# Attention in a decoder layer: four bodies written out, and each step's products regrouped (scores and maxima in front, the value product once for 512 columns)

## The reference, cut to what matters

```python
attn = jnp.einsum('bhqd,bhkd->bhqk', q, k) * scale
attn = jax.nn.softmax(attn, axis=-1)
out = jnp.einsum('bhqk,bhkd->bhqd', attn, v)
```

## Time and profile before

| | |
|---|---|
| median of 3 runs | 1193.57 us (1189.91 to 1193.67) |
| profiled execution: span from first to last instruction | 1188.0 us |
| PE busy | 1086.0 us, 91% of the span |
| DVE busy | 1021.9 us, 86% |
| ACT busy | 767.9 us, 65% |
| POOL busy | 352.7 us, 30% |
| DVE maximum reductions (line 812) | 1024, 627.1 us |
| ACT exponentials (line 750) | 512, 520.4 us |

### The profile page before, as it was taken

The page is one execution under the profiler, slowest core; times in us unless marked ns, Lnnn a source line. Parts: engine busy times, 40 slices in busy tenths (PEclk is TensorE's granted clock), DMA queues, the critical chain, the costliest instruction groups (busy, mean ns, idle before and its releaser), DMA issues. The chain is left out here.

```text
span 1188.0 us, 24515 instructions
## 1 busy us (share of the span) xinstructions
PE 1086.0 (91%) x8540; PEld 596.5 (50%) x8540; DVE 1021.9 (86%) x2168; ACT 767.9 (65%) x932; POOL 352.7 (30%) x316
## 2 busy tenths in 40 slices
PE   7889989999999998999999999999994059999998
PEld 6776333333333333333333333337784038888897
DVE  8999889999999998999999999827998975766663
ACT  4552368888888886788887888874555014655653
POOL 2657812202220220222022000022100022876575
PEclk9987699999999999999999999999998559999999
DMA  6786664504422440442344000036432022555433
GB/s 238 250 266 219 150 106 97 95 19 78 75 58 38 84 75 19 78 74 45 51 80 78 17 16 16 17 102 211 157 128 95 0 71 57 150 144 132 111 111 36
DMA packets 84695, 114.10 MB, mean 96 GB/s; under 512 B 25056, under 2 KB 57568, under 8 KB 84576
## 3 DMA queue, kind: packets, MB, share of 16 engines
q1 hardware_dynamic: 66256, 69.82, 19.8%
q0 software_dynamic: 15024, 36.17, 17.2%
q10 hardware_dynamic: 3296, 6.56, 1.6%
HBM read 73.31 MB, written 38.27 MB: 94 GB/s over the span
## 5 line engine op out<-in xcount | busy, mean ns | idle before, releaser
L812 DVE TENSOR_REDUCE b_max_halves<-banks 128x1 f32<-128x512 f32 x1024 | 627.1, 680 | 19.9 <-PE banks L880 19.7
L750 ACT ACTIVATE b_probs<-banks 128x1024 f32<-128x1024 f32 x512 | 520.4, 1026 | 153.9 <-PE banks L931 153.8
L880 PE MATMUL banks<-b_k,b_q 62*128 62x512 f32 x1024 | 399.8, 471 | 5.8 <-DVE b_max_halves L812 1.7
L931 PE MATMUL banks<-b_q,b_k 64*128 64x512 f32 x1024 | 386.9, 457 | 8.4 <-DMA b_q<-b_max_rows 5.2
L902 PE MATMUL banks<-b_probs,b_v 128*17 128x256 f32 (+1 forms) x3840 | 316.3, 402 | 0.2 <-ACT b_probs L750 0.2
L931 PEld LDWEIGHTS banks<-b_q,b_k 64*128 64x128 f32 x1024 | 157.1, 186 | 229.7 <-issue 173.3
L880 PEld LDWEIGHTS banks<-b_k,b_q 62*128 62x128 f32 x1024 | 162.2, 190 | 40.4 <-DVE b_max_halves L812 37.4
L902 PEld LDWEIGHTS banks<-b_probs,b_v 128*17 128x17 f32 x3840 | 64.0, 95 | 166.1 <-issue 99.0
L551 POOL TENSOR_TENSOR b_att<-b_out,b_rec_spread 128x512 f32<-128x512 f32 x32 | 41.0, 1283 | 307.6 <-DMA b_rec_spread<-reciprocals 307.4
L483 POOL DMA_DIRECT2D b_q<-q_stacks x60 | 31.8, 532 | 234.6 <-PE banks L902 220.9
L1851 DVE TENSOR_TENSOR e_hTl<-e_hT,e_hTh 128x512 fp32r<-128x512 f32 x64 | 47.6, 745 | 48.2 <-ACT e_hT L1605 46.6
(11 more groups left out here) (259 smaller groups left out, 1480.5 us busy)
## 6 DMA issues: line engine op xcount, KB each, us to landing
e_w<-in_w SPq DMA_DIRECT2D x16, 1024.0 KB
q_stacks<-a_parts SPq DMA_DIRECT2D x32, 256.0 KB, 4.3
k_stacks<-a_parts SPq DMA_DIRECT2D x32, 256.0 KB, 4.1
b_q<-q_stacks POOLq DMA_DIRECT2D x30, 256.0 KB, 5.7
b_k<-k_stacks POOLq DMA_DIRECT2D x30, 256.0 KB, 6.4
v_tiles<-a_v ACTq DMA_DIRECT2D x8, 544.0 KB, 3.5
b_rec_spread<-reciprocals SPq DMA_DIRECT2D x128, 32.0 KB, 1.8
attended<-b_att SPq DMA_DIRECT2D x128, 32.0 KB, 1.8
```

The source lines that it names most:

```text
L750: nc.scalar.activation(pr[:, S % NP, u], ps[:, 2 * u:2 * u + 2, :], ACT.Exp, scale=D ** -0.5).then_inc(s_ex[u], 1)
L812: v.tensor_reduce(mxp[:, (k // NB) % 2, s, p, t, kh:kh + 1], ps[:, bank(last), :], AX.X, ALU.max)\
L880: nc.tensor.matmul(ps[:, bank(last), :], qs[g][stack, p, at:at + P], ks[g][stack, p, CH * kh:CH * kh + CH], start=True, stop=True).then_in ...
L931: return nc.tensor.matmul(ps[:, 2 * u + s, :], ks[g][stack, u, P * kt:P * kt + P], qs[g][stack, u, CH * h:CH * h + CH], start=True, stop=True)
```

## The change

It does three things, in `attend` alone.

1. `bodies` writes all four batch rows out in Python; no loop is left on any engine.
2. `values` loses its `half`: each step's value product is one group for all 512 columns, for step S - 1, at the end of step S.
3. The order in a step becomes: both scores of u = 0; four maxima; both scores of u = 1; the value product of the step before; then, once in a head group, the transposed maxima as before.

```diff
         def bodies(eng, body):
-            body(0, True, False)
-            with eng.Fori(1, B - 1) as i:
-                body(i, False, False)
-            body(B - 1, False, True)
+            for i in range(B):
+                body(i, i == 0, i == B - 1)
...
-            def values(i, S, half):
+            def values(i, S):
...
-                if kt == 0 and half == 0:
-                    return
                 if kt == 0:
                     pe.wait_ge(s_oe, 8 * i + hg)
-                if kt == 0 or half == 0:
-                    for u in range(2):
-                        pe.wait_ge(s_ex[u], 64 * i + S + 1)
-                at = slice(0, CH) if kt == 0 else slice(HC * half, HC * half + HC)
+                for u in range(2):
+                    pe.wait_ge(s_ex[u], 64 * i + S + 1)
                 for j in range(G):
-                    last = nc.tensor.matmul(ps[VW * j:VW * j + VS, PV, at], vs[hg // 2][:, kt, j, :],
-                                            pr[:, S % NP, j // 2, j % 2, at], start=(kt == 0),
-                                            stop=(kt == KT - 1 and half == 1))
-                if half:
-                    last.then_inc(s_pv, 1)
+                    last = nc.tensor.matmul(ps[VW * j:VW * j + VS, PV, :], vs[hg // 2][:, kt, j, :],
+                                            pr[:, S % NP, j // 2, j % 2, :], start=(kt == 0), stop=(kt == KT - 1))
+                last.then_inc(s_pv, 1)
...
-                def earlier(S, back, half):
-                    if S >= back:
-                        values(i, S - back, half)
+                def earlier(S):
+                    if S:
+                        values(i, S - 1)
                     elif not first:
-                        values(i - 1, KT * NH + S - back, half)
+                        values(i - 1, KT * NH - 1)
...
+                        pe.wait_ge(s_ex[0], 64 * i + S)
+                        for s in range(2):
+                            last_score = scores(g, h, S, 0, s)
+                        last_score.then_inc(s_st[0], 1)
                         for u in range(2):
-                            pe.wait_ge(s_ex[u], 64 * i + S)
-                            scores(g, h, S, u, 0)
                             for x in range(2):
                                 ring(hg, kt, u, x)
-                            scores(g, h, S, u, 1).then_inc(s_st[u], 1)
-                            if u == 0:
-                                earlier(S, 2, 1)
-                            else:
-                                earlier(S, 1, 0)
+                        pe.wait_ge(s_ex[1], 64 * i + S)
+                        for s in range(2):
+                            last_score = scores(g, h, S, 1, s)
+                        last_score.then_inc(s_st[1], 1)
+                        earlier(S)
                         ring(hg, kt, 2, 0)
             bodies(pe, body)
-            values(B - 1, KT * NH - 2, 1)
-            values(B - 1, KT * NH - 1, 0)
-            values(B - 1, KT * NH - 1, 1)
+            values(B - 1, KT * NH - 1)
```

## The result

The changed kernel takes 1340.29 us (median of 4 runs, 1338.24 to 1341.19), beside 1191.74 us before (4 runs; the forecast started from the first three, 1193.57): a ratio of 1.125 (95% interval 1.122 to 1.127), 149 us more. The forecast was 1339.

A forecast was written before the change was run, and what follows sets the result against it. The prediction took PE as the bound by a hair, DVE right behind. Terms +155 - 8.5 - 3 + 2 = +145 us on 1188.0 gave 1333.5, with 5.6 to the median 1339 us; range 1308 to 1370.

The forecast's parts named there:

- What bounds the kernel before: Plain half-step of the attention stage: PE needs 1.21 us, DVE 1.19; the loop's body costs nothing, only its ends.
- The chain of the ring: Three banks tie PE and DVE: reduction and hand-over 0.75, scores 0.65, value product 0.98, next scores 0.77; 3.15 us a step.
- cross-check: The same wait already seen once in the kernel before, 2.71 us, to which the change adds score pairs of 0.22 and 0.24.
- A head group: 8 steps of 3.15 plus 0.26 for transposed maxima: 25.4 us against 20.3, +5.1; over 30.5 groups +155 us.
- The sum: All terms together +145 us on the profiled 1188.0, so 1333.5; with 5.6 to the median, 1339 us.
- Last twelve steps: Steps without maxima: PE 1.63, ACT 1.8, step between 1.8 and 2.15 us; -2 to +2 us, taken as 0.
- Written-out bodies: Loop's jump gone, -7.1 us, entry and exit about 0.8 and 0.6: together -8.5 us, lower bound of the gain 0.
- Start of the stage: Wait for copied rows at the first head group's end mostly covered, -3 us; first steps at half clock, +2 us.
- rival 2: Clock falls as PE idles: 5.0 us a step, about 1800 us throughout, 1490 if a third of steps; chance 0.07.
- Rival 1: Three banks carry DVE over the gap, so DVE sets 20.1 us a head group: about 1176 us; chance 0.06.
- Rival 3: Scores' weights load under the waiting maximum and the value product: 2.93 us a step, about 1288 us; chance 0.08.

The follow-up runs named there:

- straight_only: Kernel before with only its four batch rows written out, its order unchanged: 1182.45 us, ratio 0.994 to the kernel before.
- half_reduce: Changed kernel whose reductions read only every second of the 512 columns: 1275.67 us, ratio 1.070 to the kernel before.
- half_values: Changed kernel whose value products do 256 of 512 columns except at kt = 0: 1254.85 and 1296.81 us; run again, median 1270.19 us.
- fourth_last: Changed kernel with a step's fourth maximum moved behind the scores of u = 1, before the value product: 1283.47 us, ratio 1.080 to the kernel before.
- maxima_apart: Changed kernel with the maxima back in two pairs, each between two scores, value product still one group: 1248.97 us, ratio 1.050 to the kernel before.
- looped: Changed kernel with the loop put back over the two middle batch rows: 1344.82 us, ratio 1.130 to the kernel before.
- four_banks: Changed kernel without the second score product of u = 1, its bank given to the ring: 1200.07 and 1210.13 us, ratio 1.011 to the kernel before.

## Why the prediction was right, point by point

- **What bounds the kernel before** (PE by a hair, DVE right behind, the loop's body free): `straight_only` keeps 20.3 us a head group, so written-out code neither helps nor hurts inside a batch row. That is shown. That PE and not DVE sets the pace is read from 1.21 and 1.19 us a half-step, and no run tells the two apart.
- **The chain of the ring.** The prediction's four terms were 0.75, 0.65, 0.98 and 0.77; the profile has 0.75, 0.67, 0.99 and 0.77 (3.15 against 3.17 a step between the exponentials). The prediction's own cross-check, 2.71 + 0.22 + 0.24, gives 3.17; it did not ask where the 0.02 between the two lay. The terms were then moved: the reduction by -0.27 (`half_reduce`, step -0.27), the value product by -0.43 (`half_values`, step -0.43), the scores' place by -0.22 (`fourth_last`, step -0.24), and both pairs of scores with the maxima's places in `maxima_apart` (2.70 forecast and measured). A fourth bank takes the tie away (20.95 us a head group, nearly DVE's pace). Shown.
- **A head group**: 25.4 forecast, 25.58 measured; 5.27 more than before instead of 5.1 is, over 30.5 head groups, 5 us more than I had. The 0.26 us for the transposed maxima are right (3.42 us in that step). Among the large terms this is the only one that was off by anything that shows.
- **The sum.** On the spans it was +145 forecast and 1339.4 - 1188.0 = 151.4 measured, so the terms together were 6 us too low, 5 of them the chain's 0.02 us a step. That the median came within 1.3 us is partly luck: the kernel before has 5.6 us between its profile's span and the median that I used, the changed kernel only 0.9 (1340.29 - 1339.4).
- **Last twelve steps** at 0: from the start of the last but one head group to the last copy of the value bank it is 39.2 us after (906.3 to 945.5) and 36.1 before (758.7 to 794.8), and four of its steps with maxima explain 4 x 0.72 = 2.9 of the 3.1. Right.
- **Written-out bodies** at -8.5: in the changed kernel's profile every head group at the end of a batch row has the plain length (25.6 us at 317.9 and at 522.5), so all of the 8.5 was got, but not all of it by writing the bodies out. In `straight_only` the gain is 6.3 in the medians, because there the ends keep 0.6 us each, by the wait in `free` shown above. `looped` has plain ends with the loop in place: it is the new order that takes these 0.6 us away, and the loop's own share is the 7.8 us at its jump. That they vanish into the time in which DVE is idle anyway is argued, not shown.
- **Start of the stage** at -1 in all, which is about what it was, by other amounts. The first exponential came 3.9 us earlier (131.3 for 135.2), and the 1.3 us that the second head group had over a plain one went. The first head group took 33.1 us for 24.6, 3.2 more than the 5.3 of any other, though the wait of 2.9 us for the copied rows vanished from it: half clock lasted until 154.5 us of the span, over almost five steps of 5.0 us and not one or two. -3.9 - 1.3 + 3.2 = -2.0. These steps, by PE's timeline:

```profile
138.85 0.79 PE L923 MATMUL banks<-b_q,b_k 64*128 64x512 f32 x2
...
140.85 0.79 PE L878 MATMUL banks<-b_k,b_q 62*128 62x512 f32 x1 [0.36 <-DVE b_max_halves L810]
...
142.00 1.91 PE L896 MATMUL banks<-b_probs,b_v 128*17 128x512 f32 x8
143.84 0.79 PE L923 MATMUL banks<-b_q,b_k 64*128 64x512 f32 x2
```

From scores to scores it is 4.99 us; rival 2 had priced a step at half clock at 5.0.
- **Rival 1** (the ring does not tie) is refuted for this ring, and `four_banks` shows a condition under which it nearly holds (four banks, and one score product less). **Rival 3** (weights loaded under the waiting maximum, 2.93 a step) did not happen: the step is 3.17. What did happen in its direction is a change of partner: the score on the other rows of the array is issued together with the fourth maximum (405.07, in the timeline of the changed kernel), the one on the same rows after it. The block still takes two pairs' time.
- **Rival 2** (the clock) did not happen in the plain steps, but it is near: with a value product half as long TensorE stayed at half clock until 279 us of the span, 125 us longer than in the changed kernel's profile. Its chance of 0.07 was not too much.

## What to carry to other kernels

When a consumer on another engine is as busy as the producer, the buffers between them must last through the longest thing that the producer does in one piece. Three banks give DVE 3 x 0.60 = 1.8 us of work from the moment a bank is free. The next product that it can start on arrives 0.07 + 0.67 + 0.99 + 0.77 = 2.50 us after that moment in the changed kernel and 0.07 + 0.43 + 0.98 + 0.54 = 2.02 in `maxima_apart`, and DVE's idle times, measured as 0.68 and 0.22, are these differences to within 0.02. Before grouping a producer's work "to save its switches", write down the cycle from the buffer that frees itself to the next buffer filled, with every instruction that stands behind the waiting one in the queue; here it gave the step to within 1%. The best of the kernels tried is the one that takes only the written-out bodies, 1182.5 us.

## What the runs showed of the hardware that was not expected

- **The granted clock's rise is not tied to the program's progress.** At the start of the same stage it rose between 139 and 155 us in nine of the ten profiles of the other kernels (in `half_reduce` at 129.5, with a fall from 139.7 to 146.6 behind it); with the value product halved it rose at 279 us in one execution and near 175 in another, and the kernel's six times spread from 1247 to 1297 us. Five of these six runs have a mean granted clock of 0.899 to 0.942, lower than any run of another kernel here (0.944 and more). That makes the halved value product the likely reason; by what it would act is not shown. At half clock (1.2 GHz) a plain head group of it took 34.3 us, at full clock (2.4 GHz) 22.6.
- **Products of the same kind but other rows overtake in effect:** of two scores issued behind a waiting maximum, the second one in the program, which uses the free rows, starts with the maximum (405.07), and the first one, which shares its rows, 0.34 us later (405.41). So it is in each of the 210 such pairs whose records the trace has between 180 and 850 us of the span. The overtaking is in the starts alone: the second score's semaphore counts up at 405.83, 0.26 us after its own modelled end and 0.02 after the first one's, so who waits for it still finds both done.
- **A change between kinds of products has a price of its own, and the number of instructions none that shows:** a value product of 256 columns between other kinds of products takes 0.56 us, two in a row 0.98, and one of 512 columns with half as many instructions also 0.98.
